# A graph attention layer on one core: the residual made block by block on ScalarE and TensorE

## The reference, cut to what matters

```python
h = jnp.maximum(_layernorm(x, axis=-1), 0.0)             # x: 8192 x 256
# in the layer, with x = h, 8 heads of 32, adj 8192 x 8192 and sparse:
h = (x @ W.T).reshape(n, H, D)
attn = s_src[:, None, :] + s_dst[None, :, :] + adj[:, :, None] * We[:, 0] + be
attn = softmax(leaky_relu(where(adj > 0, attn, -inf)), axis=1)
h_out = einsum('ijh,jhd->ihd', attn, h).reshape(n, H * D)
return h_out + x @ Wr.T + br
# and outside: x = x + layer(h, adj)
```

## Time and profile before

| | |
|---|---|
| median of 3 runs | 2309.33 us (2308.79 to 2314.66) |
| the profiled execution | 2312.84 us |
| its span, first to last instruction | 2310.8 us |
| busy: VectorE (DVE) / GpSimd (POOL) | 2024.3 / 1595.9 us |
| busy: ScalarE (ACT) / TensorE matmul (PE) | 1115.5 / 1002.1 us |
| mean granted TensorE clock | 0.691 |
| DMA | 473.62 MB, mean 205 GB/s |

### The profile page before, as it was taken

How to read it: one execution, slowest core, us unless ns; L and a number is a source line. 1 busy time by engine, 2 the same in 40 slices (tenths; PEclk the granted TensorE clock), 3 DMA queues, 4 the chain that set the end, 5 groups by cost and what they waited for, 6 DMA issues and landing times. The chain is left out here.

```text
span 2310.8 us, 22965 instructions
## 1 busy us (share of the span) xinstructions
PE 1002.1 (43%) x3773; PEld 789.3 (34%) x3774; DVE 2024.3 (88%) x5351; ACT 1115.5 (48%) x4803; POOL 1595.9 (69%) x2020
## 2 busy tenths in 40 slices
PE   4767304522453194236332643353253336363343
PEld 3555203322432173225321532242242225242232
DVE  5899797899699789999888999999999998887942
ACT  2333205633574384446543654545354446485553
POOL 5544476777776777677777777777677774777775
PEclk9998656766675667667765766666666667676676
DMA  6444876667466757877777777777778885667333
GB/s 148 161 148 138 290 229 160 200 213 236 131 212 213 223 159 235 251 236 228 219 218 222 225 254 229 249 250 247 247 256 242 257 249 174 203 197 217 88 76 65
DMA packets 164570, 473.62 MB, mean 205 GB/s; under 512 B 35888, under 2 KB 54360, under 8 KB 164216
## 3 DMA queue, kind: packets, MB, share of 16 engines
q1 hardware_dynamic: 86088, 278.11, 36.6%
q0 software_dynamic: 78336, 194.09, 30.6%
HBM read 435.24 MB, written 36.83 MB: 204 GB/s over the span
## 5 line engine op out<-in xcount | busy, mean ns | idle before, releaser
L626 POOL DMA_INDIRECT arena<-table,arena x1262 | 1270.7, 1007 | 479.2 <-issue 322.1
L1347 PE MATMUL banks<-arena,ident 128*128 128x264 f32 x1566 | 500.2, 492 | 1161.9 <-DVE arena L939 1161.9
L1215 ACT ACTIVATE arena<-arena 128x32 f32<-128x32 f32 x3832 | 819.3, 307 | 2.2
L1347 PEld LDWEIGHTS banks<-arena,ident 128*128 128x128 f32 x1566 | 385.0, 251 | 1273.7 <-issue 1050.9
L772 DVE FIND_INDEX8 work<-work,adj_sb 128x8 uint32<-128x502 f32 (+56 forms) x775 | 667.2, 865 | 0.0
L783 DVE MAX8 work<-adj_sb 128x8 f32<-128x502 f32 (+56 forms) x775 | 652.4, 856 | 0.0
L1209 ACT ACTIVATE arena<-pre 128x104 f32<-128x104 f32 (+22 forms) x81 | 23.3, 304 | 910.1 <-DVE pre L929 909.6
L1353 PE MATMUL banks<-arena,ident 128*128 128x264 f32 x958 | 254.4, 408 | 42.5 <-ACT arena L1215 42.5
L939 DVE TENSOR_TENSOR arena<-arena 128x1024 f32<-128x1024 f32 (+8 forms) x169 | 226.4, 1389 | 51.3 <-ACT arena L1209 51.2
L1353 PEld LDWEIGHTS banks<-arena,ident 128*128 128x128 f32 x958 | 181.7, 197 | 103.6 <-ACT arena L1215 76.2
L1192 ACT ACTIVATE pre<-arena,we_all 128x13 f32<-128x13 f32 (+26 forms) x536 | 165.3, 406 | 87.3 <-DMA arena<-lists 87.0
(11 more groups left out here) (130 smaller groups left out, 966.2 us busy)
## 6 DMA issues: line engine op xcount, KB each, us to landing
adj_sb<-in_adj_dram SPq DMA_DIRECT2D x505, 512.0 KB, 4.4
arena<-table,arena POOLq DMA_INDIRECT x1262, 3.8
table<-arena POOLq DMA_DIRECT2D x32, 264.0 KB, 2.7
arena<-in_x_dram SPq DMA_DIRECT2D x32, 256.0 KB, 2.9
resid<-arena POOLq DMA_DIRECT2D x32, 256.0 KB, 2.6
out_dram<-arena POOLq DMA_DIRECT2D x32, 256.0 KB, 2.8
adj_sb<-in_adj_dram SPq DMA_DIRECT2D x1, 1536.0 KB, 23.5
lists<-arena,rank POOLq DMA_INDIRECT x67, 3.9
```

Of the source, the lines that this page charges most:

```text
L626: pool.indirect_dma_start(gath[0:n, un.slot(k), :], None, table[:, :], bass.IndirectOffsetOnAxis(ap=rec[0:n, k, 0:1], axis=0)).then_inc(la ...
L1215: last = s.activation(g, g, ACT.Copy, scale=gath[:, un.slot(k), HD + h:HD + h + 1])
L1347: last = m.matmul(ps_sum[:, u % 2, :], ident[:, :], gath[:, un.slot(k), :], start=(k == 0), stop=False)
```

## The change

The residual leaves the x stage. VectorE, POOL and TensorE's `maps` no longer make it. ScalarE loads x a second time, block by block, each block's relu, turn, product and write following one another on ScalarE and TensorE, which now adds x (by the identity) and br (by a row of ones) in PSUM. 24 blocks stand ahead of unit 0's exponentials, and 8 each behind the exponentials and weights of units 0 to 4; the last two steps stand behind unit 4 too. mean and deviation of all units are kept. The buffers for this lie in cells 76 to 85 of the ring, so the ring has 76 cells for its first four laps. `x_free` goes: the next load of x waits for `centre` alone. `count` and `place` of the windows and their `ranks` stand ahead of the last units' work, and POOL waits for the table's writes after it has dealt and loaded the first lists.

```diff
+LAPS = (76, 76, 76, 76)
+RES_AT = (24, 8, 8, 8, 8, 8)
...
     for un in units:
-        un.ring = at
+        un.cells = []
+        for _ in range(un.K):
+            un.cells.append(at)
+            at += 1
+            if at == (laps[0] if laps else GSLOTS):
+                at, laps = 0, laps[1:]
...
+        ps_turn, ps_res = banks[:, 3, 0:HD], banks[:, 7, 0:HD]
...
+        xr_sb = part(3 * IN).rearrange("p (u n) -> p u n", u=3)
+        hr = part(2 * IN).rearrange("p (u n) -> p u n", u=2)
+        hrT = part(2 * IN).rearrange("p (u n) -> p u n", u=2)
+        rt_sb = part(2 * HD).rearrange("p (u n) -> p u n", u=2)
...
             def load_x(u):
                 if u >= 4:
-                    sp.wait_ge(S["x_free"], u - 3)
+                    sp.wait_ge(S["hn_done"], u - 3)
...
                     pool.dma_start(by_unit(table[PAD:PAD + N, :], u), hd_sb[:, q, :, 0:ROW]).then_inc(S[f"hd_out{q}"], 16)
-                    pool.wait_ge(S["res_done"], u + 1)
-                    nc.gpsimd.tensor_tensor(rt_sb[:, q, :, :], rt_sb[:, q, :, :],
-                                            br_all.unsqueeze(1).to_broadcast([P, 2, HD]), ALU.add
-                                            ).then_inc(S["br_added"], 1)
-                    pool.wait_ge(S["br_added"], u + 1)
-                    pool.dma_start(by_unit(resid, u), rt_sb[:, q, :, :]).then_inc(S[f"res_out{q}"], 16)
-                    pool.dma_start(by_unit(out, u), rt_sb[:, q, :, :]).then_inc(S[f"res_out{q}"], 16)
-            for b in range(2):
-                for q, each in (("hd_out", 16), ("res_out", 32)):
-                    pool.wait_ge(S[f"{q}{b}"], each * (UNITS // 2))
-
-            pool.wait_ge(S["pad_out"], 16)
...
                 for k in range(un.K):
+                    if un.free_at[k] is None and un.cells[k] == LAPS[0]:
+                        pool.wait_ge(S["res_out0"], 32 * UNITS)
+                        pool.wait_ge(S["res_out1"], 32 * UNITS)
...
             deal(groups[0])
             load_dealt(groups[0])
+            for q in range(2):
+                pool.wait_ge(S[f"hd_out{q}"], 16 * (UNITS // 2))
+            pool.wait_ge(S["pad_out"], 16)
+            pool.wait_ge(S["s_done"], UNITS)
...
                 v.tensor_tensor(s_all[:, bass.ts(u, 2), :], hd_sb[:, q % 2, :, ROW:ROW + H],
                                 be_all[:, :].unsqueeze(1).to_broadcast([P, 2, H]), ALU.add).then_inc(S["s_done"], 1)
-                if u >= 2:
-                    dve.wait_ge(S[f"res_out{q % 2}"], u // 2 * 32)
-                for b in range(2):
-                    last = v.scalar_tensor_tensor(out=rt_sb[:, q % 2, b, :], in0=ps_res[:, q % 2, b, :],
-                                                  scalar=rstd[:, q, b:b + 1], in1=x_sb[:, q, b, :],
-                                                  op0=ALU.mult, op1=ALU.add)
-                last.then_inc(S["res_done"], 1)
-                dve.wait_ge(S["res_done"], u + 1)
-                dve.sem_inc(S["x_free"], 1)
...
                 windows_beside(u)
+                if u == UNITS - 2:
+                    count(groups[0])
                 scales(u, u % 4)
                 if u >= 2:
                     add_biases(u - 2, (u - 2) % 4)
+            place(groups[0])
             add_biases(UNITS - 2, 2)
-            count(groups[0])
             add_biases(UNITS - 1, 3)
-            place(groups[0])
+            dve.wait_ge(S["rstd_done"], UNITS)
+            v.tensor_tensor(shift[:, :, :], nmean[:, :, :], rstd[:, :, :], ALU.mult).then_inc(S["shifted"], 1)
...
+            def load_again(r):
+                act.dma_start(xr_sb[:, r % 3, :], x[bass.ts(r, P), :]).then_inc(S[f"xr_in{r % 3}"], 16)
+
+            def residual_step(r):
+
+                if r < TILES:
+                    act.wait_ge(S[f"xr_in{r % 3}"], 16 * (r // 3 + 1))
+                    if r >= 2:
+                        act.wait_ge(S["hr_turned"], r - 1)
+                    s.activation(hr[:, r % 2, :], xr_sb[:, r % 3, :], ACT.Relu, bias=shift[:, r // 2, r % 2:r % 2 + 1],
+                                 scale=rstd[:, r // 2, r % 2:r % 2 + 1]).then_inc(S["hr_done"], 1)
+                if 1 <= r <= TILES:
+                    act.wait_ge(S["hr_turned"], r)
+                    if r >= 3:
+                        act.wait_ge(S["res_ps"], r - 2)
+                    s.activation(hrT[:, (r - 1) % 2, :], ps_turn, ACT.Copy).then_inc(S["hrT_done"], 1)
+                if r >= 2:
+                    act.wait_ge(S["res_ps"], r - 1)
+                    if r + 1 < TILES:
+                        load_again(r + 1)
+                    if r >= 4:
+                        act.wait_ge(S[f"res_out{r % 2}"], 32 * (r // 2 - 1))
+                    s.activation(rt_sb[:, r % 2, :], ps_res, ACT.Copy).then_inc(S["res_copied"], 1)
+                    act.wait_ge(S["res_copied"], r - 1)
+                    act.dma_start(out[bass.ts(r - 2, P), :], rt_sb[:, r % 2, :]).then_inc(S[f"res_out{r % 2}"], 16)
+                    act.dma_start(resid[bass.ts(r - 2, P), :], rt_sb[:, r % 2, :]).then_inc(S[f"res_out{r % 2}"], 16)
...
+            for r in range(3):
+                load_again(r)
+            act.wait_ge(S["shifted"], 1)
             prepare(units[0])
+            for r in range(RES_AT[0]):
+                residual_step(r)
             for un in units:
                 if un.u + 1 < len(units):
                     prepare(units[un.u + 1])
                 exps(un)
+                for r in range(sum(RES_AT[:un.u + 1]), sum(RES_AT[:un.u + 2])):
+                    residual_step(r)
+                if un.u + 2 == len(RES_AT):
+                    residual_step(TILES)
+                    residual_step(TILES + 1)
...
                         rows = hnT[:, q, b, c * P:(c + 1) * P]
-                        m.matmul(ps_hd[:, q, b, :], rows, w_all[:, c, 0:272], start=(c == 0), stop=(c == 1))
-                    for c in range(2):
-                        rows = hnT[:, q, b, c * P:(c + 1) * P]
-                        last = m.matmul(ps_res[:, q, b, :], rows, w_all[:, c, 272:528], start=(c == 0), stop=(c == 1))
+                        last = m.matmul(ps_hd[:, q, b, :], rows, w_all[:, c, :], start=(c == 0), stop=(c == 1))
...
+            def residual_step(r):
+
+                if r < TILES:
+                    pe.wait_ge(S["hr_done"], r + 1)
+                    if r >= 1:
+                        pe.wait_ge(S["hrT_done"], r)
+                    for c in range(2):
+                        last = m.transpose(ps_turn[:, c * P:(c + 1) * P], hr[:, r % 2, c * P:(c + 1) * P], ident[:, :])
+                    last.then_inc(S["hr_turned"], 1)
+                if r >= 1:
+                    q = (r - 1) % 2
+                    pe.wait_ge(S["hrT_done"], r)
+                    if r >= 2:
+                        pe.wait_ge(S["res_copied"], r - 1)
+                    m.matmul(ps_res, ident[:, :], xr_sb[:, (r - 1) % 3, :], start=True, stop=False)
+                    m.matmul(ps_res, ones[0:1, :], br_row, start=False, stop=False)
+                    for c in range(2):
+                        last = m.matmul(ps_res, hrT[:, q, c * P:(c + 1) * P], wr_all[:, c, :], start=False, stop=(c == 1))
+                    last.then_inc(S["res_ps"], 1)
...
             pe.wait_ge(S["hd_copied"], UNITS)
-            ranks(groups[0])
+            for r in range(RES_AT[0]):
+                residual_step(r)
             for un in units:
                 tile_sums(un)
+                for r in range(sum(RES_AT[:un.u + 1]), sum(RES_AT[:un.u + 2])):
+                    residual_step(r)
```

More of the change, by code:

```diff
@@ L148, in slots @@
     def slots(self, lo, hi):
-        at, n = (self.ring + lo) % GSLOTS, hi - lo
-        first = min(n, GSLOTS - at)
-        return [(lo, at, first)] + ([(lo + first, 0, n - first)] if n > first else [])
+        runs = []
+        for k in range(lo, hi):
+            if runs and self.cells[k] == runs[-1][1] + runs[-1][2]:
+                runs[-1][2] += 1
+            else:
+                runs.append([k, self.cells[k], 1])
+        return [tuple(run) for run in runs]
     def slot(self, k):
-        return self.slots(k, k + 1)[0][1]
+        return self.cells[k]
 class Group:
@@ L267, in gat_kernel @@
         ones = sb("ones", [P, P])
-        w_all = sb("w_all", [P, 2, 528])
+        w_all = sb("w_all", [P, 2, ROW + H])
+        wr_all = sb("wr_all", [P, 2, HD])
         eps = sb("eps", [P, 1])
@@ L557, in _ @@
             pool.memset(eps[:, :], EPS).then_inc(S["eps_set"], 1)
+            pool.memset(rest, 0.0).then_inc(S["rest_zero"], 1)
             pool.memset(a_blk, 0.0).then_inc(S["blk_zero"], 1)
@@ L1149, in centre @@
                 for b in range(2):
-                    last = s.activation(hn[:, q % 2, b, :], x_sb[:, q, b, :], ACT.Relu, bias=nmean[:, q, b:b + 1])
+                    last = s.activation(hn[:, q % 2, b, :], x_sb[:, q, b, :], ACT.Relu, bias=nmean[:, u, b:b + 1])
                 last.then_inc(S["hn_done"], 1)
@@ L1332, in _ @@
```

(2 more changed lines are left out.)

54 lines of the change are left out of this document (33 added, 21 removed).

## The result

The changed kernel takes **2362.1 us** (median of 4 runs, 2360.6 to 2364.1), against 2311.0 us (2308.8 to 2314.7) for the kernel before on the same chip: a ratio of 1.022, 95% interval 1.020 to 1.024. It is 51 us slower. The forecast was 2323 us with a range of 2274 to 2342: the sign, to which it gave a chance of 0.50, was right, the size was not, and the time lies outside the range.

The account below looks back on a forecast made before the run. VectorE bounds the x stage, then POOL's gathers the first half. Gathers start 46 us earlier, but ScalarE's steps and the ring leave +14 us: 2327 profiled, forecast 2323 us, range 2274 to 2342.

Parts of the forecast that it names:

- Steps 1 and 2: X stage: without VectorE's residual work copies end at 216.5 us, not 250.4; POOL deals 46 us earlier, gathers begin at 235.
- Step 3: Price of a residual step on ScalarE: 4.9 us beside unit 0, 4.3 later, from load, Relu and copy.
- Rival D: TensorE's clock stays at 1.2 GHz in the steps: at least 4.6 us each, R = 147 to 155; chance 0.38 with the forecast.
- Step 4: ScalarE's sum from 235 us: unit 0's exponentials 33 us late, unit 1's 13.5; break-even 4.35 us a step.
- R: Time of the 32 residual steps on ScalarE ahead of unit 1's exponentials: 152.5 us.
- R - 139: Lateness of unit 1's exponentials on ScalarE against 424.3 us before; forecast at 13.5 us.
- Step 5: Later units: units 2 and 3 10 us late, unit 4 8 late, POOL 14 late at unit 5; sum +14 us.
- The ring's price: With 76 cells, 47 of unit 5's 48 gathers wait for unit 4's first part to be summed; about 5 us.
- C: DMA engines fill up beside unit 0: 5.8 us a step, R = 178, +39 us, 2348 us; chance 0.12.
- A: Loads of x land in 2.6 us, steps take 3.4: 24 fit beside unit 0, 31 us gained, 2278 us; chance 0.33.

Follow-up runs that it names:

- e2: Changed kernel without any of the 64 residual steps and with the ring at 86 cells from the start; 2266.8 us, 0.977 of the kernel before.
- e4: Changed kernel with br added by a product over 128 rows, 127 of them zero, instead of one row; 2318.6 us, 1.002 of the kernel before.
- e1: Changed kernel without any of the 64 residual steps, ring of 76 cells for four laps kept; 2276.6 us, 0.982 of the kernel before.
- e12: Changed kernel with six buffers for the second load of x, loaded four steps ahead, one-row br product kept; 2394.4 us, 1.034 of the kernel before.
- e14: Changed kernel with br over 128 rows, four load buffers, two steps ahead, and steps spread over ScalarE's waits; 2310.1 us, 0.997 of the kernel before.
- e15: As e14, but without the 64 writes of the scratch copy of the residual; 2301.9 us, 0.993 of the kernel before.
- e5: Changed kernel with br over 128 rows and six buffers for the second load of x, loaded four steps ahead; 2352.8 us, 1.017 of the kernel before.
- e13: As e5, but the second load shares four semaphores with the first and three redundant ScalarE waits are left out; 2307.7 us, 0.996 of the kernel before.

## Why the prediction was right or wrong, point by point

- **Steps 1 and 2 held.** The deal began at 215.9 us (forecast 218.5), the lists were there at 230.1 (forecast 235), the first gather went at 231.1. e2 measures these two steps with all that follows: 45 us of span. Unit 0's rows came at 327.3, though, not at 322: its 60 gathers took 87.7 us instead of 79.7, beside the steps' transfers.
- **Step 3 failed in its TensorE side.** It put TensorE at 4.6 us a step at the lower clock, hidden behind a load of 4.9. The even steps measured 5.30. The four products take 4.35 us (337.89 to 342.24 above) where 3.8 stood in the sum, and the copy with its two handovers 0.95 instead of 0.80. Its own rows gave more than 3.8: two products in 1.03 us at the upper level make four in 2.06, twice that at the lower one is 4.1, and the step 4.9, no longer under the load's. So TensorE, not the load, set the pace wherever a load came in time, and where it came late the step cost 6 to 9 us: ScalarE's waits for a load went up to 8.15 us, while the forecast took one middle value for all. The load's own term was about right (e4, where it stands alone: 112.7 us for 24 steps, forecast 118); wrong was that TensorE would hide behind it. The Relu takes 0.60 us instead of 0.43. Together 5.5 us a step for the 24, and for the eights, by the 39.9 us between unit 0's last weight (410.7) and unit 1's exponentials less the lists, 5.0 instead of 4.3.
- **The clock.** Rival D had the right mechanism and called it "the forecast's own time". It was in truth the main term: 32 steps at 5.30 us are 170, not 147 to 155, and with the clock up (e4) the kernel comes out at 1.002 instead of 1.022. The prediction's sentence that it "just about sets the pace" at half the clock was right as a warning, and the sum then went by the load alone.
- **Step 4 held as a sum.** R was 132.1 + 39.9 = 172 instead of 152.5, and R - 139 = 33 against 29 measured at unit 1's exponentials (453.4 less 424.3), since the steps began at 233.0 and not at 241. The formula was right and its input was not.
- **Step 5 failed too.** It had units 2 and 3 10 us late and unit 4 8 late, ScalarE catching up in idle time. Measured are 31, 35 and 36 us, and 72 at unit 5, where it had 40. A step of 5.0 us makes eight of them 40 us, more than the 37 that ScalarE had to spare ahead of an exponential (e1), so nothing was caught up. Only from unit 5 to unit 8 did slack take back 25 us, which leaves the 47. The ring's price was near: 6.7 us without steps. In the kernel after GpSimd stands 65 us for cells, since VectorE and ScalarE are late.
- **Rivals.** C gave 2348, the nearest number, in the main by another road. Its sign was there, gathers 1.49 us apart in unit 0 (87.7 us for 59 gaps; it asked for more than 1.4), and with late loads a step came near its 5.8 us; but with the loads early and the clock low (e12) the 24 steps still take 123.3 of 132.3 us. The transfers' part, unit 0's gathers 14 us longer, shows most once the clock is out of the way (e14, e15). A's quick steps came true in e5 (81.3 us for 24, 3.4 a step, A's number), but not its 31 us: e13, the same steps with the short tail, gains 10 us by the ratio, with the gathers slower beside them. The range failed because D was priced inside the forecast: it costs 47 us, not nothing.

## What to carry to other kernels

Before work is moved to TensorE, look at the shape of every product: here one of 1 or 32 rows went with the granted clock at its lower level for the whole stretch, and writing it over all 128 rows, with zeros, took no longer and was worth 47 us. Price a moved step by its slowest chain at the lower clock, add something where a second chain is nearly as long and uneven, and then check that the engine which issues it has that much idle time in each place, not on average. And when two kernels differ by tens of us behind the last instruction, compare the last instructions, not the times.

## What the runs showed that was not expected

- With a product of 1 or 32 rows, one in four of the products of 256 columns, the clock stayed at 0.50 though TensorE was busy 83% of the time or more; 128 rows let it rise to 0.78 and, with early loads (e13), to 0.92.
- Three instructions more on ScalarE lengthened the end of the program from 16 to 66 us, with 38 instruction packets instead of 4.
- Beside two additions a unit on GpSimd a VectorE operation on two columns took 714 ns instead of 176, and moving 27.8 us of work off VectorE gave back nothing.
- Two chains that take turns in ending last cost more than the longer one: 132.3 us for the 24 steps, 123.3 and 112.7 with either alone.
- Two versions come out ahead of both kernels, by little: e13 at 0.996 (0.993 to 0.998) and e14 at 0.997 (0.995 to 0.999) of the kernel before. They keep the change and repair the row count, the loads and the end of the code.
